# One exponential over the four score banks of a step in place of two over two banks each

## The chip, the cores and the metric

The kernel runs on one core of a Trainium2 chip, as one program. Its engines work side by side and meet at semaphores: TensorE (PE, with its weight loads shown apart as PEld), VectorE (DVE), ScalarE (ACT), GpSimd (POOL) and SyncE (SP), which issues most DMAs. The metric is the device time of one execution in microseconds.

## The reference, cut to what matters

Eight graphs of 1024 nodes with 128 channels and a sparse adjacency pass through two layers. The first takes, for each node, the largest features over its first 25 neighbours and a linear layer. The second is a transformer layer whose attention is restricted to neighbours in either direction and to the node itself. Both are preceded by a normalisation with ReLU, and both are added to their input.

```python
def _L1_gnn_ref(x, adj, Wqkv, ...):          # 8 heads of 16 channels, N = 1024
    allowed = (adj > 0) | (jnp.swapaxes(adj, 1, 2) > 0) | eye
    q, k, v = jnp.split(x @ Wqkv.T + bqkv, 3, axis=-1)       # then split into heads
    scores = jnp.einsum('bhqd,bhkd->bhqk', q * scale, k)
    scores = jnp.where(allowed[:, None], scores, -jnp.inf)
    attn = jax.nn.softmax(scores, axis=-1)
    ctx = jnp.einsum('bhqk,bhkd->bhqd', attn, v)
    x = _layernorm(x + ctx @ Wo.T + bo, ln1_g, ln1_b)
    ff = jax.nn.relu(x @ W1.T + b1) @ W2.T + b2
    return _layernorm(x + ff, ln2_g, ln2_b)

h = jnp.maximum(_layernorm(x, axis=-1), 0.0)
x = x + _L0_gnn_ref(adj, h, L0_gnn_W, L0_gnn_b)
h = jnp.maximum(_layernorm(x, axis=-1), 0.0)
x = x + _L1_gnn_ref(h, adj, ...)
```

## The kernel before, in words

The order of the work is written out by hand for every engine. It goes by slots: one slot per graph, with some preparing slots before the first and a closing one behind the last. A slot has 32 steps (`STEPS`). A step handles one tile of 128 keys, one half of the queries (512) and one group of four heads: four units of eight steps make a graph. Beside the attention of graph g, a slot holds the closing layers of graph g - 1 (output projection, feed-forward, norms), the first layer and the projections of graph g + 1, and the neighbour lists of the graphs after that. These are put at fixed steps by tables such as `HID_AT`, `FFN_AT` and `PROJ_AT`.

The scores of a step fill four banks of the score tensor `sc`, one per head, each 128 keys by 512 queries. In `scores` (lines 1657 to 1679) PE first waits until the probabilities of the step before have been taken from all four banks (the counter `s_probs` at twice the step's number). It then issues four products of line 1672 (eight instructions each time in the profile, since the data is float32) and sixteen small products of line 1676, four per bank, which subtract a large number where no edge is. The last product of every second bank adds 1 to `s_scores`, so a step adds 2.

ACT's `exps` (lines 1463 to 1469) turns scores into probabilities, in two activations over two banks each, and each adds 1 to `s_probs`. The probabilities go to `probs`, which has two buffers, one for even and one for odd steps; the wait for `s_pv` keeps the step before last's buffer until its value products are done. `exps` is the first thing in ACT's order at every step; behind it come, at certain steps, copies out of other banks (`context_out`, `half_out`), masks (`mask_tile`, line 1480), barred tiles (`bar`, line 1461), hidden-layer activations (line 1493) and projections (line 1499).

PE's order in step i is: the scores of step i, the value products of step i - 1 (`contexts`, line 1692), and then what the tables put at that step, for example hidden-layer products (line 1748) or edge counts (lines 1602 to 1607). `rank_counts` (lines 1617 to 1620) counts node ranks for sorting the neighbour lists, once per graph, with one product, a loop of seven and a last one.

POOL's gathers of neighbour rows wait for `s_scores` at written-out values (`paced`), so that they are spread over the slots.

Of the kernel before, what the change touches and what calls it, by code (L numbers as in the profile page):

```python
# [10 lines left out]
ACT = mybir.ActivationFunctionType  # L11
# [14 lines left out]
SCALE = 1.0 / D ** 0.5  # L26
# [162 lines left out]
def program(nc, x, adj, L0_W, L0_b, Wqkv, bqkv, Wo, bo, ln1_g, ln1_b, W1, b1, W2, b2, ln2_g, ln2_b, out):  # L189
# [6 lines left out]
    with ctx:  # L196
        def sb(name, shape, dt=fp32):
            return ctx.enter_context(nc.sbuf_tensor(name, shape, dt))

        def sem(name):  # L200
            return ctx.enter_context(nc.semaphore(name))
# [79 lines left out]
        probs = sb("probs", [P, 2, GROUP, HALF])  # L281
# [21 lines left out]
        sc = ctx.enter_context(nc.psum_tensor("sc", [P, 4, HALF], fp32))  # L303
# [66 lines left out]
        s_scores = sem("scores")  # L370
        s_probs = sem("probs")
        s_pv = sem("pv")
# [80 lines left out]
        with nc.Block() as block:  # L453
# [951 lines left out]
            def _(act):  # L1405
# [56 lines left out]

                def exps(g, n):
                    i = STEPS * g + n
                    for pair in range(2):
                        act.wait_ge(s_scores, 2 * i + pair + 1)
                        if i >= 2 and pair == 0:
                            act.wait_ge(s_pv, i - 1)
                        nc.scalar.activation(probs[:, i % 2, 2 * pair:2 * pair + 2, :], sc[:, 2 * pair:2 * pair + 2, :], ACT.Exp, scale=SCALE).then_inc(s_probs, 1)  # L1469

                def context_out(g, u):
                    act.wait_ge(s_pv, STEPS * g + T * (u + 1))
# [42 lines left out]
                for s in range(-3, B + 1):  # L1515
                    g, p, f, r, l = s, s - 1, s + 1, s + 2, s + 3
                    for n in range(STEPS):
                        if live(g):
                            exps(g, n)
# [409 lines left out]
```

## Time and profile before

| | us |
|---|---|
| median of three runs | 1257.43 (1256.55 to 1258.83) |
| the profiled execution's own time | 1252.28 |
| its span, from first to last instruction | 1250.6 |
| mean granted clock of TensorE, share of full | 0.954 |

The profile describes one execution. Durations and sums come from it; its own time is below the median of the runs, so a change is best worked out as a difference. Busy shares are averages over stages that have different limits. The attention slots start at 161, 295, 458, 583, 708, 833, 958 and 1085 us, and the last scores are taken near 1210 us.

### The profile page before, as it was taken

To read this page: it belongs to the slowest core of one execution; us is meant where nothing else is said; L and a number is where in the kernel's file an instruction comes from. 1 tells how busy PE (TensorE), PEld (TensorE's weight loads), DVE (VectorE), ACT (ScalarE), POOL (GpSimd) and SP (SyncE) were. 2 spreads that over 40 slices of the span, in tenths; PEclk is the share of its full clock that TensorE was granted. 3 is DMA by queue.
4 is the path that set the end of the run, shared out by engine and by line. 5 is a ranking of instruction groups with operands and counts; after the bars stand their busy time and mean duration, and the time that the engine had idled before them with its cause. 6 is when DMAs were issued, how large, how long until landed. Compare 5 with 4: busy or idle time off the path is not lost.

```text
span 1250.6 us, 28749 instructions
## 1 busy us (share of the span) xinstructions
PE 1045.2 (84%) x10718; PEld 401.3 (32%) x10718; DVE 806.0 (64%) x3062; ACT 806.2 (64%) x1031; POOL 733.5 (59%) x741
## 2 busy tenths in 40 slices
PE   0136687688993989999999999999999999999874
PEld 0022331233331433343334333433343334332222
DVE  8866888768788487877797779775363534122323
ACT  1221257677862867788778877887678756875541
POOL 4776677566777777777777777777777520000000
PEclk9996789898997999999999999999999999999996
DMA  6533336426333434443445334431242110000000
GB/s 191 166 70 106 95 102 161 145 63 144 92 98 98 123 94 125 125 106 90 122 127 103 104 112 128 103 99 47 80 71 73 50 52 18 19 3 10 10 9 8
DMA packets 95154, 110.74 MB, mean 89 GB/s; under 512 B 17080, under 2 KB 75968, under 8 KB 94976
## 3 DMA queue, kind: packets, MB, share of 16 engines
q1 hardware_dynamic: 68352, 62.67, 16.4%
q0 software_dynamic: 22816, 44.61, 15.6%
q8 instruction: 99, 1.62, 0.6%
q10 hardware_dynamic: 3808, 1.19, 0.4%
q14 instruction: 79, 0.65, 0.2%
HBM read 91.10 MB, written 12.85 MB: 83 GB/s over the span
## 4 chain that ended last, share of the span: by engine, by line
PE 61%; ACT 12%; DVE 10%; POOL 7%; issue 6%; DMA 3%; DVEq 0%; POOLq 0%; ACTq 0%; SPq 0%
PE sc L1672 19%; PE cb L1692 12%; ACT probs L1469 11%; PE sc L1676 6%; PE m L1748 4%; PE m L1756 4%; POOL nb_low L716 3%; POOL nb_low L694 3%; PE m L1579 2%; DMA nb_low<-h_rows,lsorted 2%; PE m L1602 2%; PE sc L1714 2%; PE m L1730 1%; PE m L1607 1%; DVE agg L1016 1%
## 5 line engine op out<-in xcount | busy, mean ns | idle before, releaser
L1469 ACT ACTIVATE probs<-sc 128x1024 f32<-128x1024 f32 x512 | 496.6, 1023 | 241.7 <-PE sc L1676 239.7
L694 POOL DMA_INDIRECT nb_low<-h_rows,lsorted x474 | 468.2, 988 | 171.5 <-issue 127.3
L1692 PE MATMUL cb<-probs,va 128*17 128x512 f32 x2048 | 271.9, 600 | 4.0 <-issue 3.3
L1672 PE MATMUL sc<-q_near,k_g 32*128 32x512 f32 x1024 | 148.0, 648 | 22.6 <-ACT probs L1469 19.1
L1672 PE MATMUL sc<-q_far,k_g 32*128 32x512 f32 x1024 | 149.3, 653 | 16.9 <-ACT probs L1469 16.1
L1016 DVE TENSOR_REDUCE agg<-nb_low 128x128 f32<-128x1024 f32 (+10 forms) x58 | 96.6, 1666 | 60.9 <-DMA nb_low<-h_rows,lsorted 37.5
L1676 PE MATMUL sc<-barred,negident 32*32 32x512 bf16 x4096 | 112.3, 387 | 0.1
L830 DVE MAX8 cand<-keys 128x8 f16<-128x128 f16 x512 | 105.3, 278 | 2.2
L716 POOL DMA_INDIRECT nb_low<-h_rows,first_lists x80 | 80.1, 1001 | 41.0 <-issue 23.2
L1461 ACT ACTIVATE barred<-m 128x512 bf16<-128x512 f32 x128 | 73.3, 608 | 40.4 <-PE m L1607 40.4
L1676 PEld LDWEIGHTS sc<-barred,negident 32*32 32x32 bf16 x4096 | 35.3, 88 | 198.5 <-issue 198.5
L1480 ACT ACTIVATE m<-keys 128x1024 fp8e5<-128x1024 f16 x64 | 67.2, 1059 | 39.6 <-DVE keys L826 39.6
L826 DVE SCALAR_TENSOR_TENSOR keys<-adj_t,prio 128x1024 f16<-128x1024 int32 x64 | 78.9, 1233 | 10.5 <-DVEq L1023 6.3
L674 POOL DMA_INDIRECT pooled_rows<-agg,lsorted x56 | 58.5, 1045 | 27.2 <-issue 14.0
L1748 PE MATMUL m<-turned,w1T 128*128 128x512 f32 x128 | 65.2, 633 | 1.0 <-ACT turned L1453 1.0
L667 POOL DMA_INDIRECT neighbour_lists<-lst,rank_i x48 | 49.4, 1030 | 27.1 <-DVE rank_i L910 13.7
L1672 PEld LDWEIGHTS sc<-q_near,k_g 32*128 32x128 f32 x1024 | 40.6, 185 | 72.5 <-ACT probs L1469 45.2
L1756 PE MATMUL m<-wide_tiles,w2T 128*128 128x512 f32 x128 | 63.2, 617 | 0.0
L1672 PEld LDWEIGHTS sc<-q_far,k_g 32*128 32x128 f32 x1024 | 40.8, 186 | 65.0 <-ACT probs L1469 44.5
L694 POOL DMA_INDIRECT nb_high<-h_rows,lsorted x46 | 47.0, 1021 | 14.0 <-issue 12.2
L1692 PEld LDWEIGHTS cb<-probs,va 128*17 128x17 f32 x2048 | 34.3, 95 | 63.8 <-issue 63.1
L1493 ACT ACTIVATE wide_tiles<-m,b1c 128x512 f32<-128x512 f32 x64 | 44.0, 687 | 15.1 <-PE m L1748 13.6
(182 smaller groups left out, 1419.4 us busy)
## 6 DMA issues: line engine op xcount, KB each, us to landing
adj_t<-in_adj_dram SPq DMA_DIRECT2D x64, 512.0 KB
nb_low<-h_rows,lsorted POOLq DMA_INDIRECT x474
xh<-in_x_dram SPq DMA_DIRECT2D x8, 512.0 KB
h_rows<-xh SPq DMA_DIRECT2D x8, 512.0 KB
hl<-h_rows SPq DMA_DIRECT2D x8, 512.0 KB
x<-in_x_dram SPq DMA_DIRECT2D x16, 256.0 KB
out_dram<-h2T SPq DMA_DIRECT2D x16, 256.0 KB, 3.3
ag<-pooled_rows SPq DMA_DIRECT2D x7, 512.0 KB
```

Source lines behind the costliest of these rows:

```text
L694: pool.indirect_dma_start(out=dst, out_offset=None, in_=h_rows[0:(f + 1) * (N + 1), :], in_offset=bass.IndirectOffsetOnAxis(ap=lsorted[:, ...
L716: pool.indirect_dma_start(out=first_slots(t)[:, k, :], out_offset=None, in_=h_rows[0:(f + 1) * (N + 1), :], in_offset=bass.IndirectOffsetO ...
L826: nc.vector.scalar_tensor_tensor(out=keys[:, t, :], in0=adj_t[:, t % 2, :], scalar=0.0, in1=prio[:, :], op0=ALU.not_equal, op1=ALU.mult).t ...
L830: ch.step(nc.vector.max(cand[:, t, 8 * c:8 * c + 8], keys[:, t, c * CW:(c + 1) * CW]))
L1016: ch.link(nc.vector.tensor_reduce(a, first.rearrange("p k c -> p c k"), AX.X, ALU.max))
L1461: nc.scalar.activation(barred[:, kt, half * HALF:(half + 1) * HALF], m[:, bank, :], ACT.Relu, bias=1.0, scale=-1.0).then_inc(done, 1)
L1469: nc.scalar.activation(probs[:, i % 2, 2 * pair:2 * pair + 2, :], sc[:, 2 * pair:2 * pair + 2, :], ACT.Exp, scale=SCALE).then_inc(s_probs, 1)
L1672: nc.tensor.matmul(sc[:, a, :], k[part, :], q[part, :], start=True, stop=False)
L1676: last = nc.tensor.matmul(sc[c * SPAN:(c + 1) * SPAN, a, :], negident[b, b], barred[b, kt, qh * HALF:(qh + 1) * HALF], start=False, stop=True)
L1692: last = nc.tensor.matmul(cb[a * SPAN:a * SPAN + VW, :], va[:, u % 2, a, kt, :], probs[:, i % 2, a, :], start=(kt == 0), stop=(kt == T - 1))
L1748: nc.tensor.matmul(m[:, bank, :], w1T[:, k * P:(k + 1) * P], turned[:, half * HALF:(half + 1) * HALF], start=True, stop=True).then_inc(s_h ...
L1756: last = nc.tensor.matmul(m[:, half, :], w2T[:, k, :], hid[:, k, :], start=(k == 0), stop=(k == FC - 1))
```

## The change

`exps` waits for both counts of a step's scores at once and issues one activation over all four banks. It adds 2 to `s_probs`, so that every other wait keeps its value. The rest of the kernel is unchanged, `rank_counts` too.

```diff
                 def exps(g, n):
                     i = STEPS * g + n
-                    for pair in range(2):
-                        act.wait_ge(s_scores, 2 * i + pair + 1)
-                        if i >= 2 and pair == 0:
-                            act.wait_ge(s_pv, i - 1)
-                        nc.scalar.activation(probs[:, i % 2, 2 * pair:2 * pair + 2, :], sc[:, 2 * pair:2 * pair + 2, :], ACT.Exp, scale=SCALE).then_inc(s_probs, 1)
+                    act.wait_ge(s_scores, 2 * i + 2)
+                    if i >= 2:
+                        act.wait_ge(s_pv, i - 1)
+                    nc.scalar.activation(probs[:, i % 2, :, :], sc[:, :, :], ACT.Exp, scale=SCALE).then_inc(s_probs, 2)
```

## Rows read from the trace of the kernel before

**Rows 1.** The page, part 1: each engine's busy time, share of span, instructions.

```profile
PE 1045.2 (84%) x10718; PEld 401.3 (32%) x10718; DVE 806.0 (64%) x3062; ACT 806.2 (64%) x1031; POOL 733.5 (59%) x741
```

**Rows 2.** Busy time in stretches; after POOL the granted clock and the DMAs.

```profile
161.00:223.00 62.00, 49.91 (x654) 16.14 (x658) 49.37 (x189) 42.97 (x54) 46.51 (x47) 0.96 0.48 128
295.00:340.00 45.00, 39.50 (x429) 14.58 (x428) 34.56 (x125) 33.51 (x43) 32.09 (x33) 0.92 0.43 109
340.00:412.00 72.00, 51.50 (x465) 18.68 (x450) 55.27 (x225) 34.71 (x41) 55.12 (x53) 0.86 0.41 124
458.00:583.00 125.00, 122.98 (x1322) 46.84 (x1322) 96.06 (x371) 100.08 (x129) 96.70 (x95) 1.00 0.41 111
...
833.00:958.00 125.00, 123.00 (x1322) 46.87 (x1326) 66.83 (x217) 95.26 (x119) 92.63 (x95) 1.00 0.31 71
```

**Rows 3.** Timeline of PE and ACT from 608.6 us: start, duration, instruction [idle before, releaser].

```profile
608.67 1.14 PE L1672 MATMUL sc<-q_near,k_g 32*128 32x512 f32 x8 [0.45 <-ACT probs L1469]
609.74 0.43 PE L1676 MATMUL sc<-barred,negident 32*32 32x512 bf16 x16
610.10 1.05 PE L1692 MATMUL cb<-probs,va 128*17 128x512 f32 x8
611.09 0.26 PE L1617 MATMUL m<-abovesum,onesb 128*128 128x208 bf16 x1
611.19 0.49 PE L1619 MATMUL m<-onehot,onesb 128*128 128x182 bf16 x7
611.54 0.25 PE L1620 MATMUL m<-onehot,before 128*128 128x208 bf16 x1
612.21 0.71 PE L1672 MATMUL sc<-q_near,k_g 32*128 32x512 f32 x4 [0.42 <-ACT probs L1469]
610.22 1.94 ACT L1469 ACTIVATE probs<-sc 128x1024 f32<-128x1024 f32 x2 [1.11 <-PE sc L1676]
```

**Rows 4.** Timeline of PE and ACT from 496.6 us, a step with hidden-layer products.

```profile
498.00 1.88 PE L1748 MATMUL m<-turned,w1T 128*128 128x512 f32 x4
499.82 0.71 PE L1672 MATMUL sc<-q_near,k_g 32*128 32x512 f32 x4
496.64 1.94 ACT L1469 ACTIVATE probs<-sc 128x1024 f32<-128x1024 f32 x2 [0.76 <-PE sc L1676]
```

**Rows 5.** Line 1469, who waited for it: whole run, then 161:295, 295:458, 458:1085, 1085:1212.

```profile
  PEld sc L1672: 89.8, 137
  PEld sc L1672: 26.4, 22
  PEld sc L1672: 9.3, 15
  PEld sc L1672: 37.2, 83
  PEld sc L1672: 17.5, 18
```

**Rows 6.** Timeline of PE, windows from 609.70 that end at 609.742 and 609.764.

```profile
609.74 0.38 PE L1676 MATMUL sc<-barred,negident 32*32 32x512 bf16 x1
609.74 0.41 PE L1676 MATMUL sc<-barred,negident 32*32 32x512 bf16 x8
```

**Rows 7.** Groups of ACT: busy us, mean ns of one, idle before and releaser.

```profile
L1469 ACT ACTIVATE probs<-sc 128x1024 f32<-128x1024 f32 x512 | 496.6, 1023 | 241.7 <-PE sc L1676 239.7
L1461 ACT ACTIVATE barred<-m 128x512 bf16<-128x512 f32 x128 | 73.3, 608 | 40.4 <-PE m L1607 40.4
L1475 ACT ACTIVATE ctx_raw<-cb 128x512 f32<-128x512 f32 x32 | 19.3, 603 | 1.4 <-PE cb L1692 1.4
L1443 ACT ACTIVATE w1T<-sc 128x512 f32<-128x512 f32 x1 | 0.6, 598 | 0.0
```

**Rows 8.** The chain that ended last, from 615 us: start, duration, engine and line.

```profile
615.72 0.03 issue
615.75 1.14 PE sc L1672 x8
...
620.16 1.07 PE sc L1672 x8
```

**Rows 9.** Waits of PE's matmuls (total, times, longest us), 458:1085, then 1085:1210.

```profile
PE sc L1672 <- ACT probs L1469: 8.8, 24, 1.1
PE m L1579 <- DVE ctxn L1048: 0.9, 1, 0.9
PE cb L1692 <- issue: 0.2, 1, 0.2
PE sc L1672 <- issue: 0.2, 1, 0.2
...
PE sc L1672 <- ACT probs L1469: 8.6, 11, 1.1
```

**Rows 10.** The chain from 161 to 458 us, shares of that stretch by line.

```profile
by line: ACT probs L1469 15.5%; PE sc L1672 13.1%; issue 10.1%; POOL nb_low L694 7.6%; DMA nb_low<-h_rows,lsorted 5.4%; PE sc L1676 4.2%; PE cb L1692 3.7%; DVE cand L830 3.7%; DVE agg L1016 3.1%; DVE keys L826 2.9%; POOL neighbour_lists L66
```

**Rows 11.** Waits of POOL, whole run.

```profile
POOL nb_low L694 <- PE sc L1676: 31.3, 54, 7.7
```

**Rows 12.** The chain of the whole run, shares by line.

```profile
by line: PE sc L1672 19.4%; PE cb L1692 12.1%; ACT probs L1469 10.7%; PE sc L1676 6.5%; issue 5.7%; PE m L1748 4.4%; PE m L1756 4.3%; POOL nb_low L716 3.1%; POOL nb_low L694 2.6%; PE m L1579 2.4%; DMA nb_low<-h_rows,lsorted 1.7%; PE m L1602
```

## The prediction

> **What bounds the kernel now.** I read the totals by engine first, then the stages, then one step closely, and last the counts over all steps. The totals [rows 1] name no single bound: PE is busy for 84% of the span, DVE and ACT for 64%. The stages [rows 2] do. From 458 to 958 us PE is busy for 123.0 of every 125.0 us at a granted clock of 1.00, and one slot (one graph, 32 steps) lasts 125 us each time. Before that (161 to 458 us, the first two slots) PE is busy for 80% and its clock averages 0.86 to 0.96, because the chain of waits there also goes through gathers and DVE. After 1210 us no exponential is left.
>
> A PE that is 98% busy isn't bound by PE alone in every step. One step of the kind to look at stands in [rows 3]. PE writes the four score banks (8 products, 1.14 us), then the 16 mask products (0.43 us), then multiplies the previous step's probabilities by the values (1.05 us), then does what little else is due. ACT starts at 610.22, behind the masks, and both exponentials together end at 612.16. PE's next scores start at 612.21, having stood idle for 0.42 us, and the row names the exponential as releaser. The cycle of 3.54 us is scores and masks (1.55) plus two exponentials (1.94) plus a hand-over of 0.05. PE's spare work doesn't fill it.
>
> The other kind is in [rows 4]: behind the value products stand four hidden-layer products (1.88 us). The exponentials of that step end at 498.58, PE reaches its next scores at 499.82, and an exponential that is 0.1 us shorter or longer changes nothing there: 1.24 us of PE work covers it.
>
> How many steps are of the first kind? PE's first instruction of a step is a weight load of line 1672, and [rows 5] count how often that load was released by the exponential: 22 and 15 times in the first two slots, 83 in the five from 458 to 1085 us, 18 in the last. The whole run has 137 such loads among its 256 steps; the four stretches add up to 138, because one load at a border is counted twice.
>
> **The change part by part.** The description speaks of ranks and nine products as well. The kernel before already counts ranks by 1 + 7 + 1 products (lines 1617, 1619 and 1620 in [rows 3]), and the diff doesn't touch them, so that half costs and saves nothing. What is left is the loop over two pairs of banks, replaced by one activation over 2048 elements per partition, which adds 2 to the counter instead of 1 twice. Nothing waits for the odd value: scores wait for 2i, the value products for 2i + 2. So 512 activations become 256, and three things change in a step.
>
> *The start is later.* The first exponential used to wait only for the first eight mask products, now for all sixteen. [Rows 6] show how little that is: the first of them is 0.38 us long, the first eight together take 0.41 us, and all sixteen 0.43 us [rows 3]. They run side by side, so the second pair is complete 0.02 to 0.03 us after the first. I take 0.025. This is why the old split bought almost no overlap: the second pair of banks was ready while the first exponential had barely begun. A step in which ACT comes to its exponential late (from a mask tile or a barred tile) doesn't pay it.
>
> *The duration.* Two exponentials over 1024 elements take 1.94 us from the first start to the last end [rows 3], against 1.02 for one, so the second adds 0.92. The trace shows no activation of 2048 elements. The nearest rows are [rows 7]: 0.598 us for a copy of 512 elements out of a score bank, 1.023 for the exponential of 1024, so 0.425 for another bank of 512. Two more banks make 1.023 + 0.850 = 1.873 us. The lower end takes the mask conversion row (0.608) instead: 1.023 + 2 x 0.415 = 1.853. The upper end supposes that an exponential streams at the distance of the two exponentials, 0.92 per 1024 elements: 1.023 + 0.92 = 1.944. I take 1.873, since three rows of other functions give 0.415 to 0.425 per bank and only overlap, which the distance of 0.92 also holds, speaks for the slower rate.
>
> The row says that two neighbours overlap by 2 x 1.023 - 1.94 = 0.106 us, and a fixed part of 1.023 - 0.850 = 0.173 us goes with the second instruction, so 0.067 is the net. The Trainium skill (ScalarE: Activation LUTs, section "What ACT_TABLE_LOAD costs") states a fixed 186 ns, 0.833 ns per element for every function, and an overlap of 93 ns between neighbours. This trace agrees with the slope (0.425 per 512 is 0.830 ns) and differs slightly on the ends: by the page the pair would take 1.985 us, where the trace has 1.94. By the page's 1.892 us for 2048 elements against the traced pair the gain is 0.023 us a step, by the page's own pair it is 0.068; the rows' value lies between them.
>
> *The release of PE.* It moves by -1.94 + 0.025 + 1.873 = -0.042, say 0.04 us earlier in a step of the first kind. With the two ends of the duration: 0.062 earlier to 0.029 later. Room for it is needed: PE must be ready that much before. In the step of [rows 3] it has 0.42 us. In steps with a gap of only a few hundredths the chain still shows the scores as 1.14 us long where ACT releases them and 1.07 where PE runs on [rows 8], so about 0.07 us more is there; 0.04 fits nearly everywhere.
>
> *The sum.* From 458 us on: (83 + 18) x 0.04 = 4.0 us. Nothing else ends a wait of PE for long there: from 458 to 1085 us PE's matmuls wait 8.8 us for exponentials, 0.9 us for DVE and 0.4 for nothing that is seen, and from there to 1210 us for exponentials alone [rows 9]. In the first two slots 37 steps qualify, but time won ahead of a wait for a gather is lost in it. The chain of that stretch [rows 10] spends 15.5% of 297 us on line 1469, 46 us, which is 24 pairs of 1.94: 24 x 0.04 = 1.0 us. POOL's gathers are paced by the scores too, and waited 31.3 us for them [rows 11], so the early steps on that chain do move them. Together 5.0 us. The profiled execution of 1252.28 us (span 1250.6) becomes 1247.3; it lies 5.15 us under the median of 1257.43, and I carry the difference over: 1252.4 us, 0.40% less.
>
> ACT itself is left idle some 256 x 0.067 = 17 us more. In covered steps that is worth nothing. It moves no DMA and no queue order, and the wait for the value products of two steps earlier, which now stands behind the wait for all scores, was met long before.
>
> **The rivals.**
>
> *Only the chain counts.* The chain of the whole run has 10.7% of 1250.6 us on line 1469 [rows 12], 134 us or 69 pairs, not 125. In the others it goes through PE because the gap before the scores is a few hundredths of a microsecond. If those steps give nothing, the gain is 69 x 0.04 = 2.8, and without the first two slots 45 x 0.04 = 1.8 us: 1255.2 us. For it: gaps as short as the 0.03 us ahead of the scores at 615.75 [rows 8]. Against: the 0.07 by which the scores are longer there. By the page's 1.892 us with all 125 steps one would get 125 x 0.023 = 2.9 us, about the same time.
>
> *One long exponential costs what two did.* If the second half streams at 0.92 us, the activation takes 1.944, the whole step is 0.029 later, and 125 steps add 3.6 us: 1261.0 us, slower. It decides from a duration of 1.94 - 0.025 = 1.915 us on. For it: no row has an exponential of another size. Against: the three rows of 512 elements [rows 7].
>
> *The clock falls elsewhere.* In 295 to 340 us the granted clock averages 0.92 [rows 2]: between 2.4 and 1.2 GHz that is 2 x 0.08 x 45 = 7.2 us at the lower level, or 3.6 us of lost PE work. Shifted steps before 458 us can add such a stretch or take one away: 1252.4 plus or minus 3.6, so 1248.8 or 1256.0. From 458 us on the clock is 1.00 and PE's idle time only shrinks.
>
> **How the numbers follow.** A difference of 0.2%, about 2.5 us, is what a measurement of this kernel can tell from no change. My forecast gets 0.56, its own range 1250.5 to 1254.5; nearly all of it is faster. Only the chain: 0.18, mostly within 0.2%. One long exponential: 0.13, nearly all slower. The clock: 0.13, faster, same and slower in about equal parts. That gives faster 0.59, same 0.26, slower 0.15. The range goes from 1249.0 (the clock's good side, and 125 x 0.062 = 7.8 us at 1249.6) to 1258.5, which takes in the clock's bad side and a duration up to about 1.93, and leaves out most of the slow rival.
>
> **What would show it.** Line 1469 should have 256 rows of about 1.87 us; above 1.92 the forecast is wrong. The cycle of a step like that at 608.67 should be 3.50 instead of 3.54 us, with 0.05 from the end of the exponential to the scores. The slots from 458 us on should be about 0.7 us shorter (16 or 17 such steps), while steps with hidden-layer products keep their length. If line 1469 is 1.87 and the slots stay at 125.0, the room was missing; if the slots shrink and the total doesn't, look at the granted clock before 458 us.

## The result and the profile after

The changed kernel is slower: 1266.09 us (median of 4 runs, 1265.2 to 1267.44) against 1257.7 us for the kernel before (4 runs beside them), a ratio of 1.0072 with a 95% interval from 1.0057 to 1.0087. Run again later beside other runs of before, it was 1.0067 (1.0046 to 1.0088). The forecast was 1252.4 us.

The profiled execution took 1265.2 us. Part 1 of its page and the groups of ACT (busy us, mean ns of one, idle before and releaser) answer to [rows 1, 7]:

```profile
PE 1041.5 (82%) x10718; PEld 399.5 (32%) x10718; DVE 806.2 (64%) x3062; ACT 789.6 (62%) x775; POOL 738.7 (58%) x741
...
L1468 ACT ACTIVATE probs<-sc 128x2048 f32<-128x2048 f32 x256 | 480.7, 1878 | 280.8 <-issue 168.1 <-PE sc L1675 111.6
```

The long exponential takes 1.878 us, as forecast, and ACT is busy for 16.6 us less, as forecast. What grew is ACT's idle time before it, from 241.7 to 280.8 us, and most of it has lost its releaser: "issue" means that the view sees nothing that the engine waited for.

The same five slots as in [rows 2], each now measured from its first scores to the next slot's (start:end, length, busy time of PE, PEld, DVE, ACT, POOL, granted clock, DMA):

```profile
460.40:588.30 127.90, 123.07 (x1320) 46.82 (x1318) 97.71 (x371) 97.75 (x97) 96.92 (x96) 1.00 0.40 109
588.30:715.30 127.00, 123.06 (x1318) 46.81 (x1318) 99.32 (x371) 97.81 (x97) 94.18 (x92) 1.00 0.42 108
715.30:842.30 127.00, 123.10 (x1322) 46.87 (x1322) 98.82 (x371) 98.02 (x97) 96.44 (x95) 1.00 0.41 110
842.30:969.00 126.70, 123.05 (x1322) 46.81 (x1322) 66.16 (x217) 93.02 (x87) 92.53 (x94) 1.00 0.30 69
969.00:1097.00 128.00, 123.27 (x1308) 46.29 (x1308) 49.14 (x165) 87.44 (x81) 35.37 (x34) 1.00 0.14 39
```

PE does the same work at the same clock, but a slot that took 125.0 us takes 127. The five slots together went from 626.9 to 636.6 us. That is where the time went: +9.8 us, and +0.9 in the last slot. Of the 12.9 us by which the two spans differ, the rest (some 2 us) lies before 460 us. The profiled execution of before was probably a lucky one there: it took 1252.28 us against a median of 1257.43, and its first two slots took 296.7 us, against 297.7 to 300.8 in the twelve other traces that kept their gathers. Among these are two whose steps are shorter than before (300.2 and 300.4 us), so it isn't the longer steps that cost time there. The medians differ by 8.4 us, and by 9.3 in the later runs, so a trace of one execution is good to a microsecond or two: a second trace of the changed kernel has 637.8 us for the five slots.

A step that PE waits in, timeline of PE and ACT: first the masks and exponentials of the kernel before in the step that begins with the last scores of [rows 3], then the same step (same keys, same graph) of the changed kernel:

```profile
613.28 0.43 PE L1676 MATMUL sc<-barred,negident 32*32 32x512 bf16 x16
613.76 1.94 ACT L1469 ACTIVATE probs<-sc 128x1024 f32<-128x1024 f32 x2 [0.66 <-PE sc L1676]
```

```profile
618.23 1.14 PE L1671 MATMUL sc<-q_near,k_g 32*128 32x512 f32 x8 [0.51 <-ACT probs L1468]
619.30 0.43 PE L1675 MATMUL sc<-barred,negident 32*32 32x512 bf16 x16
619.67 1.05 PE L1691 MATMUL cb<-probs,va 128*17 128x512 f32 x8
619.92 1.88 ACT L1468 ACTIVATE probs<-sc 128x2048 f32<-128x2048 f32 x1 [0.80 <-issue]
621.86 0.71 PE L1671 MATMUL sc<-q_near,k_g 32*128 32x512 f32 x4
```

The step is 3.63 us long (618.23 to 621.86); before it was 3.54 (612.21 to 615.75). From the start of the masks to the exponential it was 613.76 - 613.28 = 0.48 us; now it is 619.92 - 619.30 = 0.62. The forecast had 0.025 more there and got 0.14. The masks' rows end at 619.73, 0.19 us ahead of the exponential, and nothing in the timeline fills that gap.

### The profile page after: what moved, and what is told of

Its sections match the earlier page's. It is cut to its first block, busy times and chain, and to the rows that moved or that the text cites. A ratio compares the mean times of both kernels' runs of the same rounds, so it can differ in the third digit from the quotient of the medians.

```text
span 1263.5 us, 28495 instructions
## 1 busy us (share of the span) xinstructions
PE 1041.5 (82%) x10718; PEld 399.5 (32%) x10718; DVE 806.2 (64%) x3062; ACT 789.6 (62%) x775; POOL 738.7 (58%) x741
## 4 chain that ended last, share of the span: by engine, by line
PE 43%; ACT 17%; issue 9%; DVE 5%; POOL 4%; DMA 1%; POOLq 0%; DVEq 0%; ACTq 0%; SPq 0%
ACT probs L1468 15%; PE sc L1671 15%; PE cb L1691 8%; PE m L1747 4%; PE m L1755 4%; PE sc L1675 4%; POOL nb_low L694 2%; PE m L1729 1%; PE m L1789 1%; PE m L1578 1%; PE m L1777 1%; PE m L1778 1%; PE m L1601 1%; POOL neighbour_lists L667 1%; PE m L1720 1%
## 5 line engine op out<-in xcount | busy, mean ns | idle before, releaser
L1468 ACT ACTIVATE probs<-sc 128x2048 f32<-128x2048 f32 x256 | 480.7, 1878 | 280.8 <-issue 168.1
L667 POOL DMA_INDIRECT neighbour_lists<-lst,rank_i x48 | 49.9, 1039 | 29.7 <-DVE rank_i L910 16.6
L1601 PE MATMUL m<-m,ident 128*128 128x512 fp8e5 x128 | 51.8, 404 | 1.0 <-DVE bias_tiles L819 1.0
```

Source lines behind the costliest of these rows:

```text
L1468: nc.scalar.activation(probs[:, i % 2, :, :], sc[:, :, :], ACT.Exp, scale=SCALE).then_inc(s_probs, 2)
```

## The experiments

The trace records, beside the instructions, when each counter was updated. In the table all times but the last two columns are medians in us from the start of a step's masks: the update that releases the exponential, the exponential's start after it, the end of all exponentials; then the length of a step that PE spends waiting (one whose next scores start within 0.1 us of the end of its exponentials; 133 to 139 of the 255 in every kernel), the five slots from 458 us on, and the ratio of times to before with its interval. "Late" counts the updates with the sixteenth mask product that came over 0.012 us after the earliest such update of that kernel, among the 160 steps of the five slots (in up to four of them the trace has no record of it).

| kernel | update | start after | end | step | late | five slots | ratio |
|---|---|---|---|---|---|---|---|
| before | 0.457 | 0.024 | 2.419 | 3.542 | 44 (not waited for) | 626.9 | 1 |
| changed | 0.550 | 0.072 | 2.500 | 3.623 | 47 | 636.6 | 1.0072 (1.0057 to 1.0087) |
| one update of 2 | 0.524 | 0.072 | 2.474 | 3.598 | 61 | 636.6 | 1.0069 (1.0048 to 1.0089) |
| value wait first | 0.550 | 0.104 | 2.533 | 3.657 | 60 | 639.7 | 1.0113 (1.0092 to 1.0134) |
| third update | 0.576 | 0.072 | 2.525 | 3.649 | 52 | 638.3 | 1.0103 (1.0083 to 1.0123) |
| two, both wait for all | 0.550 | 0.024 | 2.512 | 3.635 | 62 | 639.1 | 1.0081 (1.0060 to 1.0101) |
| probabilities by 1 | 0.550 | 0.024 | 2.451 | 3.574 | 42 | 632.3 | 1.0029 (1.0013 to 1.0045) |
| own counter | 0.550 | 0.024 | 2.451 | 3.574 | 51 | 633.6 | 1.0040 (1.0023 to 1.0056) |
| both by 1 | 0.524 | 0.024 | 2.425 | 3.548 | 57 | 630.8 | 1.0031 (1.0016 to 1.0046) |
| one and three banks | 0.424 | 0.024 | 2.386 | 3.509 | 53 (three waited for) | 625.9 | 0.9993 (0.9976 to 1.0010) |
| no gathers from graph 3 | 0.549 | 0.072 | 2.499 | 3.623 | 4 | 633.3 | one run |
| values last | 0.549 | 0.024 | 2.450 | 3.574 | 45 | 638.6 | one run |

**One update.** PE counts a step's scores once, by 2, with the sixteenth mask product:

```diff
-                        if a % 2:
-                            last.then_inc(s_scores, 1)
+                        if a == GROUP - 1:
+                            last.then_inc(s_scores, 2)
```

> The changed kernel, but PE adds 2 to the score counter once, with the last mask product, instead of 1 after the eighth and 1 after the sixteenth. In the trace of the changed kernel the first update comes 0.458 us after the start of the masks, the second at 0.550 or, in a quarter of the steps, up to 0.3 us later, and the exponential starts 0.072 us after it; before, it started 0.023 us after the first update. Theory A (the second update is held up behind the first one): the only update comes at about 0.49, late ones vanish, the step of 3.62 us falls to 3.50 to 3.56 us; 137 such steps give 8 to 16 us less than the changed kernel, 1250 to 1258 us. Theory B (the masks of the last two banks are really ready 0.09 us later): the update stays at 0.55, at most the 0.05 us of the start comes back, 1259 to 1266 us.

Neither theory was right. The only update comes at 0.524, so the sixteenth product is really complete 0.067 us after the eighth, more than twice what the rows' ends say, and an update ahead of it adds only 0.026. Late updates didn't vanish: they were 61 of 160 here, against 47 and 56 in the two traces of the changed kernel, and the time stayed at 1265.2 us.

**The order of the waits.**

```diff
-                    act.wait_ge(s_scores, 2 * i + 2)
                     if i >= 2:
                         act.wait_ge(s_pv, i - 1)
+                    act.wait_ge(s_scores, 2 * i + 2)
```

> The changed kernel, but ACT waits for the value products first and for the scores last. Theory C (the start of 0.072 instead of 0.023 us after the update is due to the wait that is checked last): start at 0.02 to 0.03 us, 137 x 0.049 = 6.7 us less, 1259 us. Theories A and B have nothing that changes here: 1266 us within 2 us.

Theory C fell: the start came 0.032 us later instead of 0.049 earlier, and the step was the longest of all. The order of the waits matters, so there is something ahead of the activation that takes time, but it isn't the last wait.

**A third update.** With the last mask product of the first bank:

```diff
+                        if a == 0:
+                            last.then_inc(s_extra, 1)
                         if a % 2:
                             last.then_inc(s_scores, 1)
```

> The changed kernel with one update more: the last mask product of the first bank adds 1 to a counter that nobody waits for. Theory A (updates are held up behind one another, about 0.09 us each): the last update comes at about 0.63 instead of 0.55 us and more of them late, 137 x 0.08 = 11 us more, 1275 to 1280 us. Theory B (completion of the masks): no change, 1266 us within 2 us.

The last update came at 0.576: 0.026 us later, and a third of what theory A wanted. The extra update itself was there at 0.424. So each earlier update holds the later ones up a little, and the greater part of the 0.093 between the eighth and the sixteenth product is the products' own.

**Two exponentials that both wait for all four banks.**

```diff
-                        act.wait_ge(s_scores, 2 * i + pair + 1)
+                        act.wait_ge(s_scores, 2 * i + 2)
```

> The kernel before with its two exponentials, but the first of them too waits for all four banks. If the loss lies in the later wait and not in the long activation (theories A and B): the start moves from 0.48 to 0.62 us behind the start of the masks, the step from 3.54 to 3.68 us, 137 x 0.14 = 19 us more than before, 1277 us, and the trace shows the same start behind the masks as the changed kernel. If the later start belongs to the activation over four banks: start as before or 0.03 later, 1258 to 1262 us. If 0.05 of it belongs to that activation: 1270 us.

The measured start lies between the two expectations, 0.573 us behind the start of the masks: 0.092 later than before, all of it the update, and only 0.024 behind that update, where the changed kernel has 0.072. The kernel took 1266.69 us, 3 less than the third expectation. A step of it, masks and exponentials (622.86 - 622.29 = 0.57):

```profile
622.29 0.43 PE L1676 MATMUL sc<-barred,negident 32*32 32x512 bf16 x16
622.86 1.94 ACT L1469 ACTIVATE probs<-sc 128x1024 f32<-128x1024 f32 x2 [0.75 <-PE sc L1676]
```

So the loss has two parts: 0.093 for the later update, which has nothing to do with the long activation, and 0.048 that only the kernels with the long activation show.

What the 0.048 is, the rows of ACT's sequencer tell. They list the instructions that hold nothing but a wait (count, then duration in ns: least, median, most), first for the kernel before, then for the changed one:

```profile
L1468 ACTq EVENT_SEMAPHORE  x254: 17/17/17, 169.5 to 1206.0; - x127
```

```profile
L1467 ACTq EVENT_SEMAPHORE  x254: 38/2062/13209, 169.5 to 1219.0; - x127
```

Before, the separate instruction takes 17 ns each time: it holds only the wait for the value products, long met, and the exponential carries the wait for the scores itself. After, it takes 2.06 us in the median: it holds both waits, and the exponential behind it none. The operands in the trace say the same: all 256 exponentials of the changed kernel add a number to the counter and carry no wait, and all 512 of the kernel before step it by one and carry the wait for the scores. That is why "issue" stands as the releaser. In the kernel with the value wait first both waits stand in such an instruction too, which is why turning them round could not help.

**Probabilities counted by 1.** The changed kernel with one edit on each side of the counter (PE's two other waits for it, `2 * i0` and `2 * i + 2`, are halved likewise):

```diff
-  nc.scalar.activation(probs[:, i % 2, :, :], sc[:, :, :], ACT.Exp, scale=SCALE).then_inc(s_probs, 2)
+  nc.scalar.activation(probs[:, i % 2, :, :], sc[:, :, :], ACT.Exp, scale=SCALE).then_inc(s_probs, 1)
...
-                        pe.wait_ge(s_probs, 2 * i)
+                        pe.wait_ge(s_probs, i)
```

> The changed kernel with the probabilities counted by 1 per step instead of by 2 (the waits of PE are halved). In the traces of the changed kernel and of the two-exponential kernels the exponential starts 0.072 us after the update that releases it where it adds 2 and its waits stand in an instruction of their own ahead of it, and 0.024 us where it adds 1 and carries the wait for the scores itself. Theory D (the step of 2 costs 0.048 us because it drives the wait out of the activation): start 0.024 us after the update, the step 3.57 instead of 3.62 us, 137 x 0.048 = 6.6 us less than the changed kernel; ratio to before about 1.002. Rival (four banks start later by themselves): no change, ratio 1.007.

Theory D held. The start is 0.024 us after the update, the step 3.574 us, the ratio 1.0029. The separate wait is back at 17 ns, and in the timeline of the same step PE's masks are the releaser again:

```profile
L1467 ACTq EVENT_SEMAPHORE  x254: 17/17/17, 168.5 to 1213.9; - x127
```

```profile
618.24 0.43 PE L1675 MATMUL sc<-barred,negident 32*32 32x512 bf16 x16
618.82 1.88 ACT L1468 ACTIVATE probs<-sc 128x2048 f32<-128x2048 f32 x1 [0.75 <-PE sc L1675]
620.75 0.71 PE L1671 MATMUL sc<-q_near,k_g 32*128 32x512 f32 x4
```

The Trainium skill (Trainium Kernel Development and Optimization, section "Key Constraints") says that counters of compute instructions must be raised by 1. The changed kernel ran with a step of 2, so no run here shows that they must; the traces show a price of it, 0.048 us ahead of each exponential.

**POOL's waits on a counter of their own.** From the kernel above; `s_scores` is now left to POOL's gathers, and ACT waits for the new `s_full`:

```diff
-                        if a % 2:
-                            last.then_inc(s_scores, 1)
+                        if a == 1:
+                            last.then_inc(s_scores, 2)
+                        if a == GROUP - 1:
+                            last.then_inc(s_full, 1)
...
-                    act.wait_ge(s_scores, 2 * i + 2)
+                    act.wait_ge(s_full, i + 1)
```

> As the kernel with probabilities counted by 1, but the counter that POOL's gathers are paced by (2 with the eighth mask product) is another than the one ACT waits for (1 with the sixteenth). So far the update with the sixteenth mask product was up to 0.3 us late in 24 to 34% of the steps, in those alone in which it fell from 0.1 before to 0.12 or from 0.4 to 0.6 us after the start of a gather; the update with the eighth never was. Theory E (POOL's waits on the same counter hold the update up): late updates vanish, some 0.04 us a step or 3 to 5 us less, ratio about 0.999. Rival (the last mask product's update is late whatever counter it goes to): late share stays at 24 to 34%, ratio 1.002 as with the probabilities counted by 1.

Theory E fell: 51 of 160 late, ratio 1.0040.

**Both counters by 1.** The kernel with probabilities by 1, and one update of 1 per step for the scores, with all of POOL's values for it halved (one of three such waits is shown):

```diff
-                        if a % 2:
+                        if a == GROUP - 1:
                             last.then_inc(s_scores, 1)
...
-                    act.wait_ge(s_scores, 2 * i + 2)
+                    act.wait_ge(s_scores, i + 1)
...
-                                pool.wait_ge(s_scores, paced(f, t, k))
+                                pool.wait_ge(s_scores, paced(f, t, k) // 2)
```

> One exponential, both counters by 1 per step: PE updates once, with the sixteenth mask product, and POOL's waits are halved. If the three terms add up (update at 0.524 us after the start of the masks, start 0.024 later, 1.877 long), the exponential ends at 2.425 us against 2.419 before: the step is 3.545 us, and what is left against before is the late updates, 137 x 0.03 to 0.05: ratio 1.003 to 1.005 if they stay, 1.000 if they vanish. The forecast of the change (a gain of 0.04 us a step) would give 0.996.

The exponential ended at 2.425 us, as expected, the step took 3.548, and the ratio of 1.0031 is the one foreseen with late updates. This is the shortest step of the kernels with one exponential: 0.006 us behind two, and the late updates on top. One of those, in the timelines of PE, ACT and POOL of this kernel:

```profile
617.21 0.43 PE L1675 MATMUL sc<-barred,negident 32*32 32x512 bf16 x16
619.87 0.71 PE L1671 MATMUL sc<-q_near,k_g 32*128 32x512 f32 x4 [0.22 <-ACT probs L1468]
617.93 1.88 ACT L1468 ACTIVATE probs<-sc 128x2048 f32<-128x2048 f32 x1 [0.91 <-PE sc L1675]
617.79 0.99 POOL L674 DMA_INDIRECT pooled_rows<-agg,lsorted  x1 [0.30 <-issue]
```

The exponential starts 0.72 us behind the start of the masks instead of 0.547, 0.14 after POOL started an indirect DMA. PE, whose other work covers the undelayed wait here, stands idle for 0.22 us before its next scores.

**No gathers.** The changed kernel; from the third graph on the counter is raised in place of each gather (and the waits count accordingly):

```diff
                         for k in range(lo, hi):
...
+                            if f >= AHEAD:
+                                pool.sem_inc(landed, 16)
+                                continue
                             pool.indirect_dma_start(out=dst, ...).then_inc(landed, 16)
```

> The changed kernel without the gathers of neighbour rows for the graphs from the third on (458 us and later hold none of them; the maxima are then taken over zeros and old rows, the rest of the work is unchanged). Read from it: the share of steps from 458 us on whose update with the sixteenth mask product comes over 0.01 us late, 26% in the changed kernel. If gathers cause the delay: nearly 0%, and the slots lose some 0.035 us in each of 100 steps, 3 to 4 us; the 0.08 us of the undelayed steps stay. Rival (something else of the middle slots, DVE's work or the loads of adjacency): the share stays near 26%.

4 late updates of 160 instead of 47, and the five slots at 633.3 us, 3.3 less, with undelayed steps unchanged at 3.623. So gathers cause the late updates, and these cost some 3.3 of the 9.8 us. (The steps of the changed kernel give the same: its 83 waiting steps in the five slots grew by 10.3 us, and 83 x 0.081 is 6.7. Against its second trace the difference is 4.5 us.) The one run took 1253.61 us, but mostly because the first two slots, shorn of gathers too, took 286.0 us instead of 299.9.

**Value products last.** From the kernel with probabilities counted by 1, `contexts(i - 1)` is moved from right behind the scores to the end of the step:

```diff
                             scores(g, n)
-                        if 0 < i <= STEPS * B:
-                            contexts(i - 1)
...
                             turn_sum(e, h)
+                        if 0 < i <= STEPS * B:
+                            contexts(i - 1)
```

> The kernel with probabilities counted by 1, with PE's value products behind the step's other products instead of right behind the masks. Read from it: if the late update belongs to the value products that follow the masks, the late share in steps with other products falls to 0 and stays at 25 to 30% in steps without; if it doesn't, it is 25 to 30% in both. The time is of less interest: within 5 us of the kernel with probabilities counted by 1.

45 of 159 late, although in all but one of these steps another product than a value product now stands right behind the masks (an edge count in 55 of them, 21 of these late). So the late update doesn't belong to the value products. The one run took 1266.43 us, 7 more than its base and outside the expected 5. Its 638.6 us in the table is no measure of the steps: one slot took 134.1 us, the other four 125.7 to 126.8. Two steps of that slot were 3.9 and 4.3 us longer than before: in the middle of their scores PE stood idle for 1.4 and 1.5 us, for nothing that the view sees, and then the granted clock was at the lower of its two levels (0.5) for 3.4 us each time. Whether the edit has to do with these waits, one run doesn't show.

**One bank and three.** Since the time follows the update that the first exponential waits for, the kernel before was cut the other way:

```diff
-                        nc.scalar.activation(probs[:, i % 2, 2 * pair:2 * pair + 2, :], sc[:, 2 * pair:2 * pair + 2, :], ...).then_inc(s_probs, 1)
+                        banks = slice(1, GROUP) if pair else slice(0, 1)
+                        nc.scalar.activation(probs[:, i % 2, banks, :], sc[:, banks, :], ...).then_inc(s_probs, 1)
...
-                        if a % 2:
+                        if a in (0, GROUP - 1):
                             last.then_inc(s_scores, 1)
```

> The kernel before with its two exponentials cut otherwise: the first over one bank, released by the fourth mask product, the second over three. If the time is set by the update that the first exponential waits for: the update with the fourth mask product comes at 0.424 instead of 0.457 us (seen where it went to a counter of its own), both together take 1.94 us as before, so the step is 0.033 us shorter, 137 x 0.033 = 4.5 us, ratio 0.9965, and the second exponential, which starts at 0.95, is hit by no late update. If only the longest activation or the number of banks counted, it would lie between before and the changed kernel, 1.000 to 1.007.

The step is 3.509 us, 0.033 shorter, as expected. In the time it could not be told from before at first, so it was run again, with the changed kernel beside it.

> The cut into one and three banks once more, since its step was 0.033 us shorter as expected but its ratio of 0.9993 had an interval of 0.17% to either side. Expected from the step: 137 x 0.033 = 4.5 us, less what is lost to waits for DVE at the ends of slots: 0.997 to 0.999. Rival (the lost part is general): 0.999 to 1.001.

> The changed kernel once more, beside the cut into one and three banks and the same runs of before. Theories A to D agree: ratio 1.006 to 1.009.

Second time: 1253.34 us against 1255.57, ratio 0.9979 (0.9966 to 0.9992). The two intervals overlap; taken together, weighted by their intervals, they give 0.16% (0.06 to 0.26), less than the 0.36% of the steps. The step in the second run's timeline of PE and ACT:

```profile
617.28 0.43 PE L1677 MATMUL sc<-barred,negident 32*32 32x512 bf16 x16
619.72 0.71 PE L1673 MATMUL sc<-q_near,k_g 32*128 32x512 f32 x4
617.73 1.94 ACT L1470 ACTIVATE probs<-sc 128x512 f32<-128x512 f32 x2 [0.63 <-PE sc L1677]
```

It is the only version here with a shorter step than both kernels and a time below theirs, if by little. Its pair of exponentials (0.598 and 1.447 us) takes the same 1.94 us as two of 1.02, and only starts earlier.

In the five slots, 83 x 0.033 = 2.7 us were to be won, and the two traces show 1.0 and 1.3. The steps of the first one tell where the rest went. 74 of the 83 waiting steps are 0.03 to 0.04 us shorter, and two others cancel out. Four are unchanged: PE reached its next scores 0.06 us after the end of the exponentials before and 0.09 after it now, so there was no room. Three at the borders of slots are 0.10, 0.30 and 0.37 us longer, because the expectation that no late update hits the second exponential fails there. That exponential now starts 0.94 us behind the start of the masks, where with two and two it was 1.40, and in these steps the update with the sixteenth product came at 1.05 to 1.32. One of the three, ACT held up between its exponentials:

```profile
834.29 0.60 ACT L1470 ACTIVATE probs<-sc 128x512 f32<-128x512 f32 x1 [0.92 <-issue]
835.11 1.45 ACT L1470 ACTIVATE probs<-sc 128x1536 f32<-128x1536 f32 x1 [0.22 <-PE sc L1677]
```

The second trace has three such steps too. Of the 77 steps that PE doesn't wait in, 75 kept their length, and two were 0.17 and 0.48 us longer, for a reason that no run isolates.

## Why the prediction was wrong

The failing step is "The start is later", where the prediction says that the second pair "is complete 0.02 to 0.03 us after the first. I take 0.025." The real lateness is 0.141 us, so the step came out 0.081 us longer where the sum said 0.042 shorter. The 0.141 has two parts, one that the prediction sized too small and one that it put at nothing ("adds 2 to the counter instead of 1 twice"); beside them stands a loss that it didn't have:

- *0.093 us: the update with the sixteenth mask product comes that much after the one with the eighth*, at 0.550 against 0.457. The prediction read the ends of the matmul rows (0.41 and 0.43), which are modelled. The update is what releases ACT, and for the eighth product it comes 0.05 us after the row's end, for the sixteenth 0.09 when it is alone and 0.115 behind another. The two-exponential kernel that waits for all shows this term alone: +0.092 at the start.
- *0.048 us: raising the counter by 2 drove the wait out of the activation.* Shown by counting by 1, which removed this term and left the update and the length of the exponential as they were.
- *Late updates.* In 47 of the five slots' steps the update that ACT now waits for comes later, by up to 0.21 us and once by 0.71. Before, the same updates were late (44 of 160, by up to 0.24 us), but the second exponential that needs them starts 0.92 us after the first and never noticed. Without gathers all but 4 are gone, and 3.3 us with them.

The sum for a step that PE waits in: 0.093 + 0.048 - 0.061 (1.877 instead of 1.938) = 0.080, measured 0.081. In the five slots 83 such steps give 6.7 us; with 3.3 for late updates that makes 10.0, measured 9.8.

The Trainium skill (Perfetto Trace Analysis, section "Tensor Engine Instruction (MATMUL, LD_WEIGHTS)") says that a matmul's end in the profile is an estimate from its size, and that its counter is pushed only when PSUM has acknowledged all bytes. The update times above agree, and it is the rule that should have stood against the 0.025.

Point by point:

- *What bounds the kernel* was right. In steps in which PE waits, the time follows the release of the exponential one for one: every kernel of the table changes its step by what the end of its exponentials changes. Steps whose exponential PE's other work covers kept their length: 75 of 77 in the five slots, to within 0.005 us.
- *The number of steps*, 137, was right, with some luck. By the distance from the end of the exponentials to the next scores it is 137 before (83 of them in the five slots) and 133 to 139 in every kernel. But the view of [rows 5] counts something else. It also names the exponential as releaser in steps in which PE comes well after its end, and it leaves out some in which PE does wait. In the kernel before, 12 of the one kind (0.38 to 0.73 us after) and 12 of the other cancelled out. For the changed kernel, with 136 waiting steps, it gives 187:

```profile
  PEld sc L1671: 134.4, 187
```

- *The duration*, 1.873 us from the rows of other functions, was right: 1.877.
- *The release of PE*, 0.05 us after the last exponential, stayed at 0.05 in all kernels.
- *The part about ranks and nine products* was right: nothing changed there.
- *The rivals.* The slower one was forecast by another mechanism (an exponential of 1.944 us) and at a smaller size; that one is refuted by the row of 1.878. The clock didn't decide: it was 1.00 from 460 us on in both. "Only the chain counts" speaks of time won, so the loss doesn't test it (all 83 waiting steps grew, each by at least 0.07 us). The cut into one and three banks does: 74 of 83 steps took the whole gain and four none, so the room was there in nearly all of them.
- *Sums and readings.* The four hidden-layer rows of [rows 4] are two products, since each float32 product shows as two rows. The gains of "only the chain counts" lead to 1254.6 to 1255.6 us, and the upper end of the range, 1258.5, is reached at a duration of 1.924 us rather than 1.93. None of this bears on the result.
- *The sentence "This is why the old split bought almost no overlap"* was wrong in the same way: the split bought 0.093 us of start and immunity from late updates (they could come up to 0.8 us late), and cost 0.061.

## What to carry to other kernels

Where one engine hands over to another in every step, work the hand-over out from when the counter is raised, not from the end of the row; if the view doesn't show it, take the distance from the producer's start to the consumer's start as the price, and expect the last of several products to be later than the rows say. Splitting a consumer so that its first part waits for little is worth it if the second part's data arrive under the first. How small the first part should be is a trade: one bank and three had a step 0.033 us shorter than two and two, but left late data 0.94 us instead of 1.40, and in three steps that was too little. Raise counters by 1 where the waiting instruction should carry its own wait; a releaser that turned into "issue" was the sign here that it didn't.

## What the runs showed of the hardware that was not expected

- The exponential's length is linear in its elements: 0.598 us for 512, 1.024 for 1024, 1.447 for 1536, 1.877 for 2048, with two neighbours overlapping by about 0.1 us.
- Sixteen mask products of 32x32 that start within 0.05 us of each other raise their counters at 0.424 (fourth), 0.457 (eighth) and 0.524 (sixteenth), each where it is the first update of the step. With an update by the fourth product the eighth's came at 0.483, and with one by the eighth the sixteenth's at 0.550, each 0.026 later.
- The update with the sixteenth product is late (a quarter to over a third of the steps) almost only where it would fall into one of two stretches about an indirect DMA of POOL, from about 0.1 us before to 0.12 us after its start and from 0.4 to 0.6 us after it, and it then comes, in most cases, at the end of that stretch. In the kernel before 40 of the 44 late ones fell there, and of the 45 that fell there 40 were late. Single updates were later still, by 0.3 to 0.8 us, mostly in the first and last steps of a slot. The updates with the fourth and eighth product were hardly ever late in the same stretches. Neither a separate counter nor other work behind the masks changed that; taking the gathers away did. Why only the last product's update is hit stays open.
